# Expert layers with seven units ahead of the first down projection, part of the weight spreads on ScalarE's queue, and statistics taken in an FFN tail

## The reference

```python
def _L2_ffn_ref(hidden_states, ...):              # L1: softmax, top 3 of 15, gelu, biases
    router_logits = xf @ router_weight.T          # 32 experts
    routing_weights = jax.nn.softmax(router_logits, axis=-1)
    _, top_idx = jax.lax.top_k(routing_weights + e_score_bias, 6)
    combine = ...                                 # token x expert weights, normalised
    gate, up = jnp.split(jnp.einsum('th,eih->tei', x, gate_up_proj), 2, axis=-1)
    y = jnp.einsum('tei,ehi->teh', jax.nn.silu(gate) * up, down_proj)
    out = jnp.einsum('teh,te->th', y, combine) + shared_out

x = x + 0.5 * _L1_ffn_ref(_layernorm(x), ...)
x = x + _L1_attn_ref(_layernorm(x), ...)
x = x + 0.5 * _L1_ffn_ref(_layernorm(x), ...)
x = x + 0.5 * _L2_ffn_ref(_layernorm(x), ...)
x = x + _L2_attn_ref(_layernorm(x), ...)
x = x + 0.5 * _L2_ffn_ref(_layernorm(x), ...)
x = x + 0.5 * _L3_ffn_ref(_layernorm(x), ...)
x = x + _L3_attn_ref(_layernorm(x), ...)
x = x + 0.5 * _L3_ffn_ref(_layernorm(x), ...)
```

## Time and profile before

| | us |
|---|---|
| median of 3 runs (lowest, highest) | 2215.95 (2211.93, 2217.01) |
| the profiled execution | 2216.96 |
| its span, first to last instruction | 2214.9 |
| TensorE, VectorE, ScalarE, GpSimd busy | 1848.5, 1669.6, 1172.2, 1065.2 |
| mean granted clock of TensorE | 0.93 of full speed |
| variance of the four expert layers (L1387) starts at | 781.33, 1003.29, 1184.04, 1518.46 |

### The profile page before, as it was taken

How to read it: one execution, slowest core, us unless ns; L and a number is a source line. 1 busy time by engine, 2 the same in 40 slices (tenths; PEclk the granted TensorE clock), 3 DMA queues, 4 the chain that set the end, 5 groups by cost and what they waited for, 6 DMA issues and landing times. The chain is left out here.

```text
span 2214.9 us, 35952 instructions
## 1 busy us (share of the span) xinstructions
PE 1848.5 (83%) x11943; PEld 1453.6 (66%) x11943; DVE 1669.6 (75%) x4281; ACT 1172.2 (53%) x2203; POOL 1065.2 (48%) x922
## 2 busy tenths in 40 slices
PE   4888877967888789977997997996996579999856
PEld 3666663746666667755775885765884467777734
DVE  6989974879999777766777776676777856777787
ACT  3777754237777665534555653334554245666332
POOL 4899851228899746542554763401664321111022
PEclk9999999979999989988998998998997879999977
DMA  4000000000000034405442542002540010000000
GB/s 124 1 1 1 1 4 9 3 1 1 1 1 1 1 74 128 117 13 125 129 118 51 146 126 63 1 0 39 138 125 29 1 50 1 2 1 1 1 1 20
DMA packets 57186, 91.47 MB, mean 41 GB/s; under 512 B 8664, under 2 KB 19736, under 8 KB 56880
## 3 DMA queue, kind: packets, MB, share of 16 engines
q1 hardware_dynamic: 57008, 89.25, 15.2%
HBM read 87.34 MB, written 1.88 MB: 40 GB/s over the span
## 5 line engine op out<-in xcount | busy, mean ns | idle before, releaser
L1047 POOL TENSOR_TENSOR unit_hid_low<-unit_hid,unit_hid_high 128x512 fp32r<-128x512 f32 x272 | 353.0, 1298 | 275.1 <-ACT unit_hid_high L1223 275.1
L806 DVE SCALAR_TENSOR_TENSOR pk_chosen<-bank,pk_least,pk_sums 128x1024 f32<-128x1024 f32 x256 | 325.1, 1272 | 46.4 <-issue 37.2
L670 ACT COPY pk_sums<-bank 128x1024 f32<-128x1024 f32 x256 | 261.0, 1021 | 125.3 <-PE bank L568 125.0
L568 PE MATMUL bank<-pk_pick,pk_sim_both 128*128 128x512 f32 x512 | 191.5, 456 | 104.8 <-DVE pk_chosen L806 104.7
L484 POOL TENSOR_TENSOR pk_chosen<-pk_chosen 128x1024 f32<-128x1024 f32 (+1 forms) x126 | 265.4, 2109 | 13.7 <-DVE pk_chosen L806 13.7
L1104 PE MATMUL bank<-unit_x_high,units_high 128*128 128x512 f32 x544 | 221.4, 407 | 22.0 <-ACT unit_gact L1216 8.3
L1105 PE MATMUL bank<-unit_x_low,units_high 128*128 128x512 f32 x544 | 216.7, 398 | 0.0
L1106 PE MATMUL bank<-unit_x_high,units_low 128*128 128x512 f32 x544 | 216.4, 398 | 0.0
L1223 ACT CAST unit_hid_high<-unit_hid 128x512 fp32r<-128x512 f32 x272 | 166.8, 613 | 64.0 <-DVE unit_hid L1371 32.0
L568 PEld LDWEIGHTS bank<-pk_pick,pk_sim_both 128*128 128x128 f32 x512 | 78.9, 193 | 162.3 <-DVE pk_chosen L806 126.0
L583 PE MATMUL bank<-ident,pk_chosen 128*128 128x128 f32 x1152 | 149.6, 276 | 0.0
(11 more groups left out here) (419 smaller groups left out, 4498.8 us busy)
## 6 DMA issues: line engine op xcount, KB each, us to landing
unit_comb<-comb_dram SPq DMA_DIRECT2D x136, 256.0 KB, 3.3
unit_comb<-comb_dram SPq DMA_DIRECT2D x272, 128.0 KB, 3.2
raw<-in_geglu_units SPq DMA_DIRECT2D x3, 774.0 KB, 7.2
raw<-in_swiglu_units SPq DMA_DIRECT2D x3, 768.0 KB, 9.6
dh_w<-in_de_w SPq DMA_DIRECT2D x1, 1024.0 KB, 6.1
out_x<-x_res SPq DMA_DIRECT2D x1, 1024.0 KB, 5.1
raw<-in_geglu_units SPq DMA_DIRECT2D x1, 967.5 KB, 10.8
raw<-in_swiglu_units SPq DMA_DIRECT2D x1, 960.0 KB, 12.7
```

The lines of the kernel that those rows point to most:

```text
L568: ins = nc.tensor.matmul(sums_ps[:, 2 * b + e, :], both[:, i % 2, h, :], pk.pick[:, e * PK_K // 2:(e + 1) * PK_K // 2, :].rearrange("p i j ...
L670: nc.scalar.copy(sums_sb[:, b, :].rearrange("p (e n) -> p e n", e=2), sums_ps[:, 2 * b:2 * b + 2, :]).then_inc(sums_out.sem, 1)
L806: nc.vector.scalar_tensor_tensor(chosen[:, h, :].rearrange("p (e n) -> p e n", e=2), sums_ps[:, 2 * b:2 * b + 2, :], least2[:, i % 2, h:h ...
L1047: nc.gpsimd.tensor_tensor(hid_low[:, i % HB, :], hid[:, i % HB, :], hid_high[:, i % HB, :].bitcast(FP32), ALU.subtract).then_inc(hidden.se ...
```

## The change

In `experts_ffn`:

- The order of TensorE. Gate 0 goes ahead of the last transposes, up 0 ahead of `turn_comb(0)`. The first downs, 0 and 1, come behind up 6, then 2 and 3 behind up 7; from step 8 on it is down i - 4 as before.
- VectorE's weightings come in lots: units 0 to 2 behind product 6, 3 to 5 behind product 7, 6 and 7, then 8 and 9. The first five products stay in `hid`, the next three in the free `k.xn`. ScalarE's roundings follow these lots.
- ScalarE's queue issues the spreads of units 1 and 3 of group 0, behind activation 2; SyncE does the others.
- `x_high` and `x_low` of groups 1 to 3 leave the prologue: ScalarE rounds them at steps 11, 22 and 33, and GpSimd subtracts. VectorE normalises all tiles of groups 2 and 3.
- GpSimd splits the new weights of nine units (before six) ahead of its first hidden split; VectorE's four come at steps 9 to 12 (before 7 to 10). The twelve tiles' combine weights all come behind product 4.
- `load_square_root` at the end is gone; the program then has its table load ahead of the root in the next block.

In `fp4_ffn` the first call takes statistics: 12 tiles ahead of the last two additions, 4 behind them; `decay_attention` then measures nothing.

```diff
+    FIRST_DOWN = 6
+    STEADY = FIRST_DOWN + 3
+    BY_ACT = (1, 3)
+    ROUND_X = {11 * g: g for g in range(1, NG)}
+    DOWN = {FIRST_DOWN: (0, 1), FIRST_DOWN + 1: (2, 3)} | {i: (i - LAG,) for i in range(FIRST_DOWN + 2, ALL + LAG)}
+    HIDE = {FIRST_DOWN: (0, 1, 2), FIRST_DOWN + 1: (3, 4, 5), FIRST_DOWN + 2: (6, 7),
+            STEADY: (8, 9)} | {i: (i,) for i in range(STEADY + 1, ALL)}
+    ROUND = {FIRST_DOWN: (0, 1), FIRST_DOWN + 1: (2, 3, 4), FIRST_DOWN + 2: (5, 6),
+             STEADY: (7, 8)} | {i: (i - 1,) for i in range(STEADY + 1, ALL + 1)}
...
-        product_of = lambda i: hid[:, i, :] if i < AHEAD else prod_ps[i % 2]
+        spare = k.xn[:].rearrange("p t d -> p (t d)")
+        product_of = lambda i: (hid[:, i, :] if i < HB else
+                                spare[:, group_of(i - HB)] if i < FIRST_DOWN + 2 else prod_ps[i % 2])
...
             turn_x(2)
+            project_gate(0)
+            turn_x(3)
             route(1)
-            turn_x(3)
             route(2)
             route(3)
+            project_up(0)
             turn_comb(0)
-            for i in range(ALL + LAG + 2):
+            for i in range(1, ALL + LAG + 2):
...
-                if LAG <= i < ALL + LAG:
-                    project_down(i - LAG)
+                for j in DOWN.get(i, ()):
+                    project_down(j)
...
+            for i in range(ALL + LAG + 1):
+                if i < ALL:
                     activate(i)
-                if new and 8 <= i + 7 < U:
-                    round_weights(i + 7, i + 8)
-                if i - 1 < ALL:
-                    round_hidden(i - 1)
+                if new:
+                    round_weights(i + 3 if i < 4 else 2 * i - 1, min(i + 4 if i < 4 else 2 * i + 1, U))
+                for j in ROUND.get(i, ()):
+                    round_hidden(j)
+                if i == 2:
+                    for j in BY_ACT:
+                        spread_comb(j)
...
-            k.load_square_root(act)
...
-                if 1 <= i < AHEAD:
-                    hide(i - 1)
-                if AHEAD - 1 <= i < ALL:
-                    hide(i)
-                if i in (4, 5, 6):
-                    weigh(i - 3)
+                if i == 4:
+                    for g in range(1, NG):
+                        weigh(g)
+                for j in HIDE.get(i, ()):
+                    hide(j)
...
+            if not last:
+                nc.vector.drain()
+                measure(k, range(NT - 2 * S))
             add(NS - 2)
             add(NS - 1)
+            if not last:
+                nc.vector.drain()
+                measure(k, range(NT - 2 * S, NT))
+    k.measured = not last
...
-        fp4_ffn(k, f4)
+        fp4_ffn(k, f4, last=False)
         decay_attention(k, a)
-        fp4_ffn(k, f4)
+        fp4_ffn(k, f4, last=True)
```

More of the change, by code:

```diff
@@ L1002, in experts_ffn @@
         logits_ps = [bank[:, 0:len(tiles) * E].rearrange("p (t e) -> p t e", e=E)
-                     for bank, tiles in ((up_ps[1], first), (gate_ps[1], rest))]
-        comb_t_ps = [bank[0:PART, :] for bank in (up_ps[1], out_ps[1], out_ps[0], out_ps[1])]
+                     for bank, tiles in ((up_ps[1], first), (norm_ps[1], rest))]
+        comb_t_ps = [bank[0:PART, :] for bank in (norm_ps[0], out_ps[1], out_ps[0], out_ps[1])]
         over = lambda a, n: a.unsqueeze(2).to_broadcast([P, n, E])
-        product_of = lambda i: hid[:, i, :] if i < AHEAD else prod_ps[i % 2]
+        spare = k.xn[:].rearrange("p t d -> p (t d)")
+        product_of = lambda i: (hid[:, i, :] if i < HB else
+                                spare[:, group_of(i - HB)] if i < FIRST_DOWN + 2 else prod_ps[i % 2])
         @block.sync
@@ L1031, in _ @@
                     store_comb(STORE[i])
-                spread_comb(i)
+                if i not in BY_ACT:
+                    spread_comb(i)
                 if i == U // 2 and load_next is not None:
@@ L1230, in read_out, with spread_comb @@
                 nc.scalar.copy(out_t[:], out_ps[g % 2]).then_inc(down_out.sem, 1)
+            def spread_comb(i):
+                if i == BY_ACT[0]:
+                    act.wait_ge(stored.sem, stored.at(16))
+                for h in range(m.halves):
+                    rows = slice(h * P // m.halves, (h + 1) * P // m.halves)
+                    c = i * m.halves + h
+                    act.dma_start(comb[rows, i, :], k.comb_dram[c:c + 1, group_of(0)]
+                                  .to_broadcast([P // m.halves, 512])).then_inc(comb_in[i].sem, 16)
             act.wait_ge(var_ready.sem, var_ready.at(1))
@@ L1276, in normalise @@
             def normalise(g):
-                for t in range(g * GT, g * GT + ACT_TILE):
+                for t in range(g * GT, g * GT + (ACT_TILE if g < 2 else GT)):
                     nc.vector.tensor_scalar(k.xn[:, t, :], k.x[:, t, :], k.mv[:, t, 0:1], rstd[:, t:t + 1],
@@ L1440, in experts_ffn @@
         sig.passed(2)
-    for sig in (xn_ready_act, transposed, copied, x_rounded, x_low_ready, comb_ready, comb_t, comb_out, down_out, turned,
+    x_low_ready.passed(1)
+    x_low_pool.passed(NG - 1)
+    xn_ready_act.passed(2)
+    for sig in (transposed, copied, x_rounded, comb_ready, comb_t, comb_out, down_out, turned,
                 added):
@@ L2547, in passed, with fp4_ffn @@
             self.k.counter(name).passed(n)
-def fp4_ffn(k, f4):
+def fp4_ffn(k, f4, last):
     nc = k.nc
```

69 lines of the change are left out of this document (33 added, 36 removed).

## The result

| | before | changed |
|---|---|---|
| median us (runs) | 2215.02 (4) | 2243.04 (4) |
| lowest, highest | 2211.93, 2217.01 | 2238.61, 2243.39 |
| profiled span | 2214.9 | 2240.8 |
| mean granted clock | 0.930 | 0.927 |

The ratio is 1.0123, 95% interval 1.0105 to 1.0141: slower by 23 to 31 us. The forecast was 32.

The account below looks back on a forecast made before the run. TensorE bounds the steady stretches; only ramps, with VectorE's products, weightings and ranking, can move. Ramps 27.3, clock 4, exits 3.5 and tail -2.5 sum to +32.3 on the median 2215.95: 2248 us, range 2222 to 2264.

Parts of the forecast that it names:

- Ramps, 27.3 plus clock 4: Four expert layers' starts grow by 27.3 us together; TensorE's longer holes lower the granted clock, 4 more (0 to 8).
- step 1: Expert layer's ramp: gate 0 and up 0 ahead of turn_comb(0) on TensorE delay it and ScalarE's copy by 2.56 us.
- Rival A: In the ramps, early gate 0 raises the granted clock sooner, saving 2 to 3 us each: +20, 2236; chance 0.20.
- Steps 2 and 3: Fourth layer's ramp: first activation 2.0 us later; VectorE's seven products take 10.9 and end at 1548.0, before any weighting.
- Steps 4 and 5: Fourth layer: TensorE waits twice for weighting, rounding and split, holes some 5 and 3.8 us; ramp grows by 5.1.
- The third layer: Third expert layer's ramp: 5.1 + 0.5 + 2 × 0.98 = 7.5 us longer, the latter terms for Pool's weight splits.
- The second layer's stall: VectorE's 7.43 us wait for unit 9's spread behind the next weights' load remains and comes 7.2 us later.
- Exits, 3.5: Behind the expert layers, the square-root table loads after the barrier: root 1.05 us late, one exit counted a third; +3.5.
- Tail, -2.5: End of the first FFN stage: twelve tiles' statistics run in earlier holes, variance 3.05 us earlier; -2.5 (0 to -3.05).
- Inputs and issuing queue, nothing: Later rounding and splitting of groups 1 to 3's inputs, and ScalarE issuing units 1 and 3: no cost or gain.
- Rival B: Mixing itself cost time before; if the first weighting starts by 1544, both trips vanish: faster, 2207; chance 0.12.
- Rival C: Spreads land so late that weights hold the first weighting either way: within 5 us of before; chance 0.06.

Follow-up runs that it names:

- the filled holes: Changed kernel plus 26 unneeded matmuls per expert layer in TensorE's waits, 104 in all; 2237.73 us, ratio 1.0107 to the kernel before.
- roots back: Changed kernel with the square-root table loaded again at the end of each expert layer; 2236.89 us, ratio 1.011 to the kernel before.
- mixing back: Changed kernel with the earlier order of weightings, downs and weight splits, all spreads by SyncE; early projections stay; 2219.45 us, ratio 1.0025 to the kernel before.
- weights split first: Changed kernel with all 13 of GpSimd's splits of new weights ahead of its first split of a product; 2239.81 us, ratio 1.0119 to the kernel before.

## Why the prediction was right

The time (2243 against 2248), the direction and the cause hold: late weightings in lots put trips over four engines on TensorE's path, and moving them back gives 20 to 22 of the 27 us. That the time came so near is partly luck, since two terms erred in opposite directions: step 1 was some 5 us too high, and the trips were 2 to 4 too low. Of the terms:

- **Ramps, 27.3 plus clock 4.** Measured 29.8 for both together. By layer, without the clock term: 7.5, 7.2, 7.5, 5.1 forecast, 8.1, 5.9, 11.3, 4.4 measured. The clock's part is 3.5 (times) to 6.0 (ramps) by the filled holes, so the trips and the copy are 24 to 26. Both are one profile's figure or a difference within the intervals.
- **Step 1 failed.** Gate 0 and up 0 were to put the copy 2.0 to 2.6 later in each layer. It came 0.6 sooner in the first and 0.7 in the fourth, 2.4 and 2.3 later in the second and third: the sum of step 1 is 3.4, not 8 to 10, and its price in time 0 to 6 us. Rival A's mechanism works in some layers and not in others. I had given it as all or nothing.
- **Steps 2 and 3 hold.** Seven products in a row take 11.1 us (forecast 10.9), and the first weighting is 14.29 behind the copy. In the fourth layer, from an earlier copy, that is 5.1 later than before (26.54 for 21.41 behind the variance).
- **Steps 4 and 5 hold in kind, not in size.** There are two trips, but the holes are 2.9 and 1.2 us, not 5 and 3.8, and ScalarE's rounding ends the larger part of the first. Gate 7 was forecast 1.7 later and came 0.6 sooner; the way from gate 7 to gate 8 was forecast 3.4 longer and is 4.9 longer, with matmuls at half clock and weightings that took more than the 0.69 I used (three in 3.25). Gate 8 came 4.2 later, forecast 5.1: a copy 3.3 sooner than forecast, and a way from there that was 2.4 longer. Step 4 also misread the kernel before: at its gate 7 (1550.68) only downs 0 to 2 were done, down 3 follows at 1552.06. The sum goes by gate 8 and doesn't change.
- **The third layer was mis-sized**, 7.5 for 11.3. The copy, 2.3 later, was in the forecast. Of the 3.8 above it, 2.6 is clock by the filled holes (0.67 over 21 us), a term that I had apart, and up to 2.2 lies on VectorE, where first product to first weighting took 13.4 us, 11.2 in the fourth layer: two wide operations of the ranking took 1.25 and 1.06 beside Pool's splits of new weights, 0.56 each there. I had that in the upper bound of 33 alone.
- **The second layer's stall**: still there (5.29 us, below), and the first weighting of unit 9 came 6.5 later behind the variance (53.09 for 46.60); 7.2 forecast.

```profile
1065.98 0.75 DVE L1401 SCALAR_TENSOR_TENSOR unit_hid<-bank,units_small,unit_comb 128x512 f32<-128x512 f32 x1 [5.29 <-DMA unit_comb<-comb_dram]
```

- **Exits, 3.5**: 3.4 in the rows; 2.9 in the times, which can't tell it from nothing. The drain of 1.38 us at a switch that the Trainium skill gives (ScalarE: Activation LUTs, What ACT_TABLE_LOAD costs) does not show here either: the root at 969.38 starts 1.30 behind the load's start at 968.08, whose own length is 1.28.
- **Tail, -2.5**: 2.8 in the stage; 2.0 in the times, between 0 and 4.2.
- **Inputs and issuing queue, nothing**: no gain or loss that the times of the two runs can tell. The Trainium skill (DMA: Bandwidth & Descriptors, Issuing engines are not separate DMA queues) says that a second issuing engine saves only the issuing time. The run with SyncE's spreads agrees, 1.0125 against 1.0123.

Rival B fell, but not by its own number. Put on the clock of the trace of before, the first weighting started at 1545.0, nearer to its 1544 than to my 1548, and unit 6 was through as much sooner, near 1544 and not 1547; so TensorE still waited. What decides is the distance between the two, not the time. Rival C fell: the first weighting waited for products and not for a transfer, and the time lay 27 us above, not within 5.

## What to carry to other kernels

Work done ahead fills a ramp only if the chain behind it (product, weighting, rounding, split) starts as early as before; weighting in lots behind the last unit made trips over four engines, and the second one, where unit 3 is weighted only behind product 7, cost most. On an in-order queue look at which instruction stands behind each new wait: here activation 2 behind a rounding, and weighting 3 behind product 7. A bulk load issued into a ramp that lives on small transfers can hold them up (7.43 us here); issued in parts in the steady stretch it made that layer 4.3 us shorter.

## What the hardware did that I had not expected

- The granted clock rises at different points of the same instruction stream: in the first layer of the changed order the copy came at 13.9 behind the variance in most kernels and at 17.0 in two with the same prologue on TensorE (roots back, mixing back). Layers with an unchanged order moved by up to 1.8 us between kernels (the second layer of weights split first). So single terms under 2 us can't be told from one profile.
- 104 useless matmuls didn't make the kernel slower, 1.0107 for 1.0123 of before (the intervals overlap), and the clock rows (1.00 for 0.64 to 0.67) and the ramps (-6.0) show what they gave back.
- Whether GpSimd slows a weighting of 128x512 on VectorE depends on where the product lies. In the changed kernel's two layers with plain weightings, all 109 that read the product from a bank with GpSimd running throughout took 0.69 us; the six that read it from `hid` or `x_norm` in the same case took 1.31 to 1.76. The change keeps eight products of each layer there, before it was four. One of each kind, with GpSimd's timeline of the same moments:

```profile
1246.13 1.52 DVE L1404 TENSOR_TENSOR unit_hid<-x_norm,unit_comb 128x512 f32<-128x512 f32 x1 [0.16 <-issue]
...
1255.20 0.69 DVE L1404 TENSOR_TENSOR unit_hid<-bank,unit_comb 128x512 f32<-128x512 f32 x1 [0.16 <-POOL unit_hid_low L1058]
```

```profile
1245.38 3.40 POOL L1058 TENSOR_TENSOR unit_hid_low<-unit_hid,unit_hid_high 128x512 fp32r<-128x512 f32 x2
...
1253.82 2.54 POOL L1058 TENSOR_TENSOR unit_hid_low<-unit_hid,unit_hid_high 128x512 fp32r<-128x512 f32 x2 [1.28 <-ACT unit_hid_high L1243]
```
